# B and C of the state-space stage: projected once and convolved on VectorE, and the causal mask moved from a sum to a product

## The reference

```
zxbcdt = layernorm(x) @ W_in.T              # z 256, x 256, B 16, C 16, dt 4
xBC    = silu(causal_conv(xBC, conv_w, 4 taps) + conv_b)   # per channel, along the sequence
A      = -exp(A_log) * softplus(dt + dt_bias)              # 4 heads
L[l,s] = exp(sum of A over s < d <= l)  for s <= l, 0 above the diagonal
Y      = sum over s <= l of (C[l] . B[s]) * L[l,s] * dt[s] * x[s]     # the chunks of 64 give the same sums
Y      = rmsnorm((Y + D * x) * silu(z)) * norm_w
out    = Y @ W_out.T
```

## Time and profile before

| what | value |
| --- | --- |
| median of 3 runs | 2781.34 us (2774.32 to 2793.9) |
| the profiled execution | 2801.32 us |
| its span, first to last instruction | 2799.5 us |
| mean granted TensorE clock in it | 0.941 of full speed |
| TensorE matmul busy | 2320.1 us, 83% of the span |
| VectorE busy | 1919.9 us, 69% |
| ScalarE busy | 1925.3 us, 69% |
| GpSimd busy | 1472.8 us, 53% |

### The profile page before, as it was taken

One profiled execution on the slowest core, in us unless ns is written; L12 is line 12 of the kernel. 1 busy time (PEld: TensorE's weight loads), 2 busy tenths in 40 slices (PEclk: granted clock), 3 DMA queues, 4 the chain that ended last, 5 costly groups with the idle time before them and its releaser, 6 DMA issues. The chain is left out here.

```text
span 2799.5 us, 46444 instructions
## 1 busy us (share of the span) xinstructions
PE 2320.1 (83%) x13516; PEld 1224.0 (44%) x13516; DVE 1919.9 (69%) x5318; ACT 1925.3 (69%) x4833; POOL 1472.8 (53%) x1308
## 2 busy tenths in 40 slices
PE   6999879989999898766776677676799898988987
PEld 3555435545555455412222222222455555555553
DVE  2332357767777676459988998998677676777764
ACT  3444358777777778576877687766687777787774
POOL 1221246555555455247777787676555555555551
PEclk9999979999999999978888888889899999999999
DMA  3000000000000000000000000000000000000000
GB/s 130 1 0 0 0 12 12 13 9 12 13 13 13 9 12 13 5 0 0 1 1 1 0 0 1 0 0 0 12 13 13 9 16 9 13 17 16 20 13 16
DMA packets 12190, 30.46 MB, mean 11 GB/s; under 512 B 2240, under 2 KB 2240, under 8 KB 11456
## 3 DMA queue, kind: packets, MB, share of 16 engines
q1 hardware_dynamic: 11968, 27.99, 3.6%
HBM read 9.11 MB, written 2.10 MB: 4 GB/s over the span
## 5 line engine op out<-in xcount | busy, mean ns | idle before, releaser
L499 POOL TENSOR_TENSOR arena<-arena 128x512 f32<-128x512 f32 x256 | 325.5, 1271 | 691.9 <-DVE arena L1451 689.6
L543 POOL TENSOR_TENSOR arena<-arena 128x512 f32<-128x512 f32 x256 | 328.1, 1298 | 123.9 <-ACT arena L1225 121.3
L1457 DVE TENSOR_REDUCE SM<-arena 128x8 f32<-128x512 f32 x256 | 175.0, 683 | 292.3 <-ACT arena L1093 286.5
L1093 ACT ACTIVATE arena<-psum 128x512 f32<-128x512 f32 x256 | 152.4, 595 | 253.3 <-PE psum L821 249.3
L512 POOL TENSOR_TENSOR P<-P,RS 128x512 f32<-128x512 f32 x256 | 270.2, 1056 | 98.8 <-DVE RS L1383 96.6
L892 PE MATMUL psum<-BS,tabs 96*128 96x512 bf16 x384 | 144.4, 437 | 208.6 <-DVE arena L1534 207.1
L1534 DVE TENSOR_TENSOR_SCAN arena<-arena,psum 128x512 f32<-128x512 f32 x256 | 310.9, 1215 | 3.2
L961 PE MATMUL psum<-arena,first 128*128 128x512 f32 x512 | 290.4, 656 | 11.2 <-POOL arena L534 10.9
L821 PE MATMUL psum<-rest,HA 128*128 128x512 f32 x512 | 273.5, 616 | 11.7 <-DVE arena L1451 10.6
L505 POOL TENSOR_TENSOR arena<-arena,SR 128x512 f32<-128x512 f32 x256 | 275.2, 1075 | 7.4 <-ACT SR L1103 6.5
L774 PE MATMUL psum<-HN,rest 128*128 128x512 f32 (+1 forms) x384 | 195.0, 620 | 94.6 <-DVE arena L1418 45.6
(11 more groups left out here) (222 smaller groups left out, 5816.5 us busy)
## 6 DMA issues: line engine op xcount, KB each, us to landing
arena<-arena SPq DMA_DIRECT2D x128, 128.0 KB, 2.3
rest<-in_rest SPq DMA_DIRECT2D x1, 4183.0 KB, 22.6
X<-in_x SPq DMA_DIRECT2D x1, 2048.0 KB, 10.6
out<-X SPq DMA_DIRECT2D x8, 256.0 KB, 2.2
first<-in_first SPq DMA_DIRECT2D x1, 1445.5 KB, 6.2
tabs<-in_tabs SPq DMA_DIRECT2D x1, 1216.0 KB, 13.1
```

Of the source, the lines that this page charges most:

```text
L499: nc.gpsimd.tensor_tensor(CQ[:, n % 2, :], CQ[:, n % 2, :], SQN[:, n % 2, :], ALU.add).then_inc(f_rope, 1)
L543: nc.gpsimd.tensor_tensor(WU[:, k % DEEP, :], RG[:, k % DEEP, :], U[t.j % 2][:, k % 2, :], ALU.mult).then_inc(m_wu, 1)
```

## The change

B and C are projected without taps, in one f32 matmul (two instructions) instead of four. VectorE then applies the four taps to the 48 x 512 result, out of PSUM into a new tile `BCT`, a tensor_scalar and three scalar_tensor_tensors on shifted ranges, each waiting for the one before (`conv_bc`, half-turn 12, behind `MM` of that half-turn). ScalarE's silu of B and C reads `BCT` and waits for the last tap.

The causal mask leaves the segment sums. It is now a table of ones and zeros, which VectorE multiplies into the product of C and B, once for each sequence, from PSUM into a new tile `CBM` in SBUF (`masked`, half-turns 0 and 2). `MM` is made from `LM` and `CBM`. The product of the second sequence moves from half-turn 8 to half-turn 2 on TensorE, since its bank is free as soon as the first is masked. The transposes of half-turn 14 wait for the last tap, as they write the bank that the taps read.

```diff
@@ segsum
-                mm(seg[:, 0:384], T16("ident16"), T16("causal"), start=True, stop=False)
-                mm(seg[:, 0:128], AM[:, q % 2, 0, :], F("le"), start=False, stop=False)
-                mm(seg[:, 128:256], AM[:, q % 2, 0, :], F("ones"), start=False, stop=False)
-                mm(seg[:, 128:256], AM[:, q % 2, 2, :], F("le"), start=False, stop=False)
-                mm(seg[:, 256:384], AM[:, q % 2, 1, :], F("le"), start=False, stop=True).then_inc(a_seg, 1)
+                mm(seg[:, 0:128], AM[:, q % 2, 0, :], F("le"), start=True, stop=True)
+                mm(seg[:, 128:256], AM[:, q % 2, 0, :], F("ones"), start=True, stop=False)
+                mm(seg[:, 128:256], AM[:, q % 2, 2, :], F("le"), start=False, stop=True)
+                mm(seg[:, 256:384], AM[:, q % 2, 1, :], F("le"), start=True, stop=True).then_inc(a_seg, 1)
@@ c_times_b
-                t.wait_ge(a_mm, 8, 4 * b)
+                t.wait_ge(a_cm, 2, b)
@@ a_pe_beginning
                 elif h == 11:
                     t.wait_ge(a_act, 6, 1, pair=1)
-                    conv(t, slice(256, 304), X_BANK[0][0:48, :], 0)
-                    conv(t, slice(256, 304), X_BANK[0][0:48, :], 2)
+                    mm(X_BANK[0][0:48, :], win_bc[:, :], XN[:, :, 3:3 + SEQ], start=True, stop=True).then_inc(a_z, 1)
...
                 elif h in (14, 15):
                     part = h - 14
-                    t.wait_ge(a_act, 6, (4, 5)[part], pair=1)
+                    if part:
+                        t.wait_ge(a_act, 6, 5, pair=1)
+                    else:
+                        t.wait_ge(a_act, 6, 2, pair=1)
+                        t.wait_ge(a_cv, 4, 4, pair=1)
@@ a_pe_turn
-                        if h == 8:
+                        if h == 2:
                             c_times_b(t, 1)
@@ a_act_beginning
-                        t.wait_ge(a_z, 5, 3, pair=1)
+                        t.wait_ge(a_cv, 4, 4, pair=1)
                         rows = slice(32 * k, 32 * k + NS)
-                        A(dst[side][:, :], X_BANK[0][rows, :], ACT.Silu, bias=F("a_convb_bc")[rows, :]).then_inc(a_act, 1)
+                        A(dst[side][:, :], BCT[rows, :, :].rearrange("p b t -> p (b t)"), ACT.Silu, bias=F("a_convb_bc")[rows, :]).then_inc(a_act, 1)
@@ block.vector, ahead of the stage
             for c in range(CONV):
-                TT(convW[:, c, 0:272], F("a_win", 256, 528), F("a_convw", 288 * c, 288 * c + 272), ALU.mult)
-                TT(convW[:, c, 288:304], F("a_win", 528, 544), F("a_convw", 288 * c + 272, 288 * c + 288), ALU.mult)
-                v.memset(convW[:, c, 272:288], 0.0)
+                TT(convW[:, c, :], F("a_win", 256, 512), F("a_convw", 256 * c, 256 * c + 256), ALU.mult)
+            TS(win_bc[:, 0:16], F("a_win", 512, 528), 1.0, None, ALU.mult)
+            v.memset(win_bc[:, 16:32], 0.0)
+            TS(win_bc[:, 32:48], F("a_win", 528, 544), 1.0, None, ALU.mult)
@@ new on VectorE
+            def conv_bc(t):
+                src = pair(X_BANK[0][0:48, :])
+                t.wait_ge(a_act, 6, 4)
+                t.wait_ge(a_z, 5, 3, pair=1)
+                TS(BCT[:, :, :], src, F("a_convc", 3, 4, p=48), None, ALU.mult).then_inc(a_cv, 1)
+                for i in range(1, CONV):
+                    t.wait_ge(a_cv, 4, i, pair=1)
+                    STT(BCT[:, :, i:], src[:, :, 0:SEQ - i], F("a_convc", 3 - i, 4 - i, p=48), BCT[:, :, i:],
+                        ALU.mult, ALU.add).then_inc(a_cv, 1)
+
+            def masked(t, b):
+                t.wait_ge(a_cb, 2, b + 1)
+                t.wait_ge(a_mm, 8, 4 * b + 4, pair=-1)
+                TT(CBM[:, b, :], CB_BANK[:, 0:384], T16("causal"), ALU.mult).then_inc(a_cm, 1)
@@ a_dve_beginning
+                elif h == 12:
+                    conv_bc(t)
@@ a_dve_turn
-                        t.wait_ge(a_cb, 2, q // 4 + 1)
+                        if h in (0, 2):
+                            masked(t, h // 2)
+                        t.wait_ge(a_cm, 2, q // 4 + 1)
                         t.wait_ge(a_lm, 8, q + 1)
                         t.wait_ge(a_y, 8, q - 1)
-                        TT(MM[:, q % 2, :], LM[:, q % 2, :], CB_BANK[:, 0:384], ALU.mult).then_inc(a_mm, 1)
+                        TT(MM[:, q % 2, :], LM[:, q % 2, :], CBM[:, q // 4, :], ALU.mult).then_inc(a_mm, 1)
```

More of the change, by code:

```diff
@@ L47 @@
     ("ident", 128), ("mean128", 128), ("mean256", 128), ("ones", 128), ("le", 128), ("strict", 256),
-    ("a_win", 548), ("a_convw", CONV * 288), ("a_convb", 2), ("a_convb_bc", 1), ("a_dtb", 16),
+    ("a_win", 548), ("a_convw", CONV * 256), ("a_convc", CONV), ("a_convb", 2), ("a_convb_bc", 1), ("a_dtb", 16),
     ("a_alog", 16), ("a_d", 2), ("a_normw", 2), ("a_wout", 2 * 128)])
@@ L159, in program @@
         SEG_BANK, Y_BANK, CB_BANK, X_BANK = (bank[0], bank[1]), (bank[2], bank[3]), bank[4], (bank[6], bank[5])
-        convW = shared("ssd", [128, CONV, 304])
+        convW = shared("ssd", [128, CONV, 256])
+        win_bc = shared("ssd", [128, 48])
+        BCT = shared("ssd", [48, 2, SEQ])
+        CBM = shared("ssd", [128, 2, 384])
         XN = shared("ssd", [128, 2, SEQ + CONV - 1])
@@ L175, in program @@
         a_cb = sem("a_cb")
+        a_cm = sem("a_cm")
+        a_cv = sem("a_cv")
         a_am = sem("a_am")
@@ L1659, in shape_tables @@
             sel[32 * part + s, s, :] = 1.0
-    b = {"ident16": np.eye(128), "band": np.where(band, 0.0, MASKED), "causal": np.where(causal, 0.0, MASKED),
+    b = {"ident16": np.eye(128), "band": np.where(band, 0.0, MASKED), "causal": np.where(causal, 1.0, 0.0),
          "sel": sel.reshape(128, 32 * 128)}
@@ L1687 @@
     f.update({
-        "a_win": A["W_in"].T, "a_convw": np.tile(A["conv_w"][:, 0, :].T.reshape(1, -1), (128, 1)),
+        "a_win": A["W_in"].T, "a_convw": np.tile(A["conv_w"][:256, 0, :].T.reshape(1, -1), (128, 1)),
+        "a_convc": np.pad(A["conv_w"][256:, 0, :].reshape(2, NS, CONV), ((0, 0), (0, 32 - NS), (0, 0))).reshape(64, CONV),
         "a_convb": cols(A["conv_b"][:256, None], 2), "a_convb_bc": np.pad(A["conv_b"][256:].reshape(2, NS), ((0, 0), (0, 32 - NS))).reshape(64, 1),
```

## The result

The kernel became slower. Its median is 2814.2 us (2813.0 to 2827.3) against 2784.9 us of the kernel before on the same chip: ratio 1.0107, 95% interval 1.0077 to 1.0137. A second measurement on another chip, among the experiments, gave 1.0099 (1.0079 to 1.0118). The forecast was 2779, 2761 to 2795.

A forecast was written before the change was run, and what follows sets the result against it. Matmuls were taken to bound the first stage nearly everywhere, except at two TensorE holes fed by chains through other engines. 4.1 us gained less 1.5 for the clock left 2.6, from 2781.3 to 2779 us; range 2761 to 2795.

The forecast's parts named there:

- The step that failed: At TensorE's 2.02 us hole ahead of the next pair's mean: one more clock fall in the stage, 1.5 us lost.
- the tail: From half-turn 11's start to head 7's product in each turn: 10.24 us before, 10.40 forecast.
- rival C: First stage: TensorE loses its clock in every turn's tail until after `L617`; 3.5 us a turn, 2802 us; chance 0.07.
- Part 1, the masks: Segment sums on TensorE: each 0.17 us shorter without its mask; 0.86 us a turn for five, plus 0.17 at the start.
- Part 2, the taps: B and C in the tail: TensorE saves 2.60 us a turn, VectorE's four taps take 3.10; no gain.
- Buy nothing: The 2.60 us a turn TensorE saves on B and C gain no time; z's wait becomes the taps' wait.
- Part 3, the mask on VectorE: `masked` in half-turns 0 and 2, 0.56 us each, fits into existing waits: no time lost.
- Part 4, the shared port: `MM` with two SBUF inputs blocks against GpSimd: 0.4 us a turn lost at the start, 0.25 in the tail.
- The sum without the clock: First stage: 0.4 us gained in each of seven turns, 1.4 in the last; 4.1 us together.
- Rival A: First stage: TensorE is the bound and all it loses counts; 32 us, 2749 us; chance with its half 0.10.

The follow-up runs named there:

- the start filled: Changed kernel plus six products a turn that nobody reads, only ahead of the next pair's mean; 1.0044 of the kernel before.
- the filled kernel: Changed kernel plus sixteen f32 products a turn that nobody reads, where TensorE waits in the tail and ahead of the next pair's mean; 0.9986 of the kernel before.
- the kernel before, filled: Kernel before plus ten products a turn that nobody reads, 8 ahead of the mean, 2 ahead of head 7's product; 0.9996 of the kernel before.
- the two halves: Changed kernel with only B and C's taps on VectorE, 1.0021 of the kernel before; with only the causal mask on VectorE, 1.0004.

## Why the prediction was wrong

**The step that failed** is "With 2.6 us more idle time just ahead of this hole I count one more: -1.5". That is one fall more of the kind that the kernel before has, behind the hole and over within 3 to 4 us. In fact the clock fell in the tail itself, where no idle stretch was as long as the 2 us hole, and stayed down through the start of the next turn. It did so in two turns of the first profile and four of the second. The lower level took 77 and 108 us of the stage instead of some 20. The mechanism stood in the text as rival C, at 2802 us and a chance of 0.07, with the argument against it that "in the tail no idle stretch is as long as that one". This argument was the mistake: it looked for one long wait, and the fall at 160.7 stands behind waits of 0.32 and 1.32 us only (those of 0.88 and 1.55 come while the clock is down). With the start filled, the tail's waits alone bring a fall in every turn. They do not always: in the next tail of the first profile the same two, and one of 1.42 behind them, brought none before the next turn (1.00 until 212). The Trainium skill ("TensorE: Matmul & The Clock Gate", "A second HAM failure mode: psum-queue depth-cycling") describes the nearest case: a bf16 kernel in which TensorE idles briefly but often between groups of matmuls and its clock swings between the two levels. The trace agrees in the swings, 1.00 and 0.50 above, behind idle stretches of 0.3 to 1.4 us. The prediction drew on the section about long gaps instead.

**The size of C.** It put 3.5 us a turn on work at half speed on the path. From head 7's product to `L621` it is 8.37 instead of 5.97, 2.40, in such a turn, and the slow sums behind `L621` come on top. The five turns lost 11.7 us, the last one and its ending 5.7, the first 0.9: 18.3 in the first pair of profiles.

**Part 1, the masks**: right in sign, mis-sized. A segment sum was to shrink by 0.17 us with its mask. TensorE alone, one sum of the changed kernel, and the row of the kernel before that follows the two in the earlier trace rows:

```profile
135.23 0.49 PE L586 MATMUL psum<-first,arena 128*128 128x128 f32 x2
135.55 0.39 PE L587 MATMUL psum<-first,arena 128*128 128x128 f32 x2
135.78 0.39 PE L588 MATMUL psum<-first,arena 128*128 128x128 f32 x2
```

```profile
136.66 0.39 PE L583 MATMUL psum<-first,arena 128*128 128x128 f32 x2
```

The first product now takes 0.32 to the next one's start, the second 0.23. Before, mask and first product took 0.17 + 0.22 = 0.39 together, so a mask is worth 0.07 us: the five on the path 0.35 instead of 0.86. The likely reason, not tested, is that the first product now pays for its own weights: in the kernel before their load starts with the mask (136.27), 0.17 ahead of the product that uses them, here with the product itself (135.23).

**Part 2, the taps**: right. Projection, `MM`, taps, ScalarE and product fall where the sum had them; the four taps take 3.06 us (154.85 to 157.91), 3.10 forecast, the tail 10.49, 10.40 forecast. One small thing went the other way: B and C take ScalarE 1.47 us out of SBUF, not 0.1 less than the 1.39 out of PSUM. "Buy nothing" is what the filled kernel shows, whose turns at the full clock are no shorter than before's.

**Part 3, the mask on VectorE**: as forecast in the turn at 207 to 213: `masked` ends at 209.68 (0.56 us), and `MM` of head 0 at 210.73 still waits for the exponential, 1.05 us.

**Part 4, the shared port**: seen, smaller than taken. `MM` in groups, before (35.5 us, mean 555 ns) and after:

```profile
L1364 DVE TENSOR_TENSOR arena<-arena 128x384 f32<-128x384 f32 x64 | 37.7, 589 | 166.6 <-PE psum L608 123.1 <-ACT arena L1057 43.5
...
L1307 DVE SCALAR_TENSOR_TENSOR arena<-psum,first,arena 48x510 f32<-48x510 f32 (+2 forms) x24 | 17.7, 738 | 0.8
```

The longest took 797 ns. All 64 lost 2.2 us together, where 0.65 us a turn had been put on the path; `MM` of head 6 in the tail lost 0.23 (0.79 at 154.14), as taken. At the start `MM` of head 0 lost 0 (0.56 at 210.73) or 0.2, not 0.4. The chain from the product of head 7 to `L621` at full clock, which has two lengths turn about, is 5.63 and 5.97 us in the filled kernel and 5.78 and 5.94 before: 0.06 shorter on average, where 0.23 longer was worked out.

**The sum without the clock** is not borne out in its parts. It had 0.4 us gained in each turn. Two turns in a row at the full clock take 77.77 us in the filled changed kernel (82.67 to 160.44) and 77.88 before (82.84 to 160.72), 0.05 a turn: masks of 0.35, a start of 0.06 and a tail of -0.25 make 0.16. The whole time, 0.9986 of before, would be 4 us where 4.1 was worked out, but its interval also holds 0, and the stage of the filled changed kernel ends 2.2 us after that of the kernel before, filled: this agreement is luck. Rival A was rightly kept small: the tail did not shrink. The 1% within which 0.91 of the chance was placed was passed by the first measurement by a hair, in the direction that had 0.03.

**What stays open**: why the two halves cost 0.2% and 0% alone and 1.0% together, or, as the traces have it, why only the changed kernel has turns in which the clock stays down for 17 us; and why the same waits bring a fall in one turn and none in the next. That the clock answers to idle time is shown by the filling; how the short waits add up to a fall is not.

## What to carry to other kernels

When matmuls are taken out of a stretch that TensorE does not bound, the time between them is not free: read the granted clock of the stretch, count the short waits around it and not the longest alone, and put a price on the lower level for what lies on the path. Before such a change, move the work that takes the matmuls' place to where its engine waits anyway, as far ahead of its reader as the buffers allow: here the same taps five half-turns earlier turned +1.0% into -0.3%. Cheap filling products at the waits are a test of the cause in one run, and in this case a gain of a further 0.6%. Hold a slow turn against a fast one of the same place in the loop: here two lengths alternate.

## What the runs showed of the hardware

Busy time can hide half speed: TensorE was busy for 2320 us in both kernels, with 112 instructions and some 25 us of work less in the second (8 x 2.60 and 64 x 0.07). In the turn shown the clock fell behind waits of 0.32 and 1.32 us and stayed down for some 17 us, through head 7's product and the next turn's start; the 2.40 us that this cost between the two is more than either wait. The same waits in the next turn brought no such fall. The share of a stage at the lower clock varied from one execution of a kernel to another: 13.6 and 23.8 us before, 77.3 and 108.2 after.
